# Two-layer kernel: C rows by DMA, the modulation product on GpSimd, and the last addition moved to the next stage

## What is computed

```python
h = layernorm(x) * (1 + ca) + sa
x = x + ga * state_space(h)
h = layernorm(x) * (1 + cb) + sb
x = x + gb * experts(h)
```

```python
h = exp(dt * A) * h + dt * u * B      # a scan over the 1024 tokens
y = sum_n(h * C) + u * D
out = (y * silu(z)) @ W_out.T + residual
```

## Time and profile before

| | us |
|---|---|
| median of 3 runs (4103.15 to 4108.57) | 4107.88 |
| span of the profiled execution, first to last instruction | 4108.2 |
| busy: TensorE, VectorE, ScalarE, GpSimd | 3305.6, 3549.2, 2321.0, 2624.4 |
| state-space stage, first scan to the last store | 2098.7 to 3914 |
| experts stage, first load to the end | 3918.9 to 4108 |

### The profile page before, as it was taken

The page is one execution under the profiler, slowest core; times in us unless marked ns, Lnnn a source line. Parts: engine busy times, 40 slices in busy tenths (PEclk is TensorE's granted clock), DMA queues, the critical chain, the costliest instruction groups (busy, mean ns, idle before and its releaser), DMA issues. The chain is left out here.

```text
span 4108.2 us, 61159 instructions
## 1 busy us (share of the span) xinstructions
PE 3305.6 (80%) x21708; PEld 1529.2 (37%) x21708; DVE 3549.2 (86%) x5829; ACT 2321.0 (56%) x4302; POOL 2624.4 (64%) x2459
## 2 busy tenths in 40 slices
PE   5979999999993999999566777777777777776467
PEld 3633333333332555555322232222232232222166
DVE  5768888888854999999359999999999999999967
ACT  5626666666672344444356666666666666666422
POOL 1102323232232888888369999999999999998723
PEclk8969999999996999999888888888888888887689
DMA  4894565655513111110112222212222222222132
GB/s 146 281 188 64 78 84 79 88 80 81 82 33 89 35 44 45 44 48 30 34 44 61 63 65 64 69 47 60 69 65 64 65 69 61 68 57 53 42 95 85
DMA packets 274957, 299.58 MB, mean 73 GB/s; under 512 B 35583, under 2 KB 205686, under 8 KB 274646
## 3 DMA queue, kind: packets, MB, share of 16 engines
q1 hardware_dynamic: 274654, 295.68, 31.4%
HBM read 210.22 MB, written 84.51 MB: 72 GB/s over the span
## 5 line engine op out<-in xcount | busy, mean ns | idle before, releaser
L1727 POOL TENSOR_TENSOR d_dBu<-d_dtu,d_Bn 128x1024 f32<-128x1024 f32 x512 | 1217.5, 2413 | 0.1
L1562 ACT ACTIVATE d_dA<-d_dt,d_decay 128x512 f32<-128x512 f32 x1024 | 690.9, 687 | 404.4 <-DVE d_h L1810 402.1
L752 ACT ACTIVATE b_P<-b_pT 128x512 f32<-128x512 f32 (+1 forms) x1120 | 571.8, 575 | 298.1 <-PE b_pT L658 295.3
L1810 DVE TENSOR_TENSOR_SCAN d_h<-d_dA,d_last_h,d_dBu 128x512 f32<-128x512 f32 x512 | 617.1, 1265 | 14.5 <-ACT d_dA L1562 12.8
L1810 DVE TENSOR_TENSOR_SCAN d_h<-d_dA,d_dBu 128x512 f32<-128x512 f32 x512 | 586.3, 1204 | 40.3 <-ACT d_dA L1562 39.0
L785 DVE CUSTOM_DVE_ANT_0 b_pS<-b_pS,mask_qk 128x512 f32<-128x512 f32 (+1 forms) x768 | 501.7, 690 | 83.6 <-PE b_pS L668 74.3
L630 POOL TENSOR_SCALAR_AFFINE_SELECT b_P<-b_P 128x128 f32<-128x128 f32 (+2 forms) x608 | 192.8, 321 | 515.0 <-ACT b_P L752 503.2
L668 PE MATMUL b_pS<-KS,QS 99*128 99x512 bf16 (+3 forms) x1536 | 475.0, 339 | 28.5 <-PEq L85 21.6
L658 PE MATMUL b_pT<-QS,KS 118*128 118x512 bf16 (+3 forms) x1536 | 449.1, 329 | 3.1 <-ACT b_P L752 2.1
L1817 DVE TENSOR_TENSOR d_h<-d_h,d_C 128x2048 f32<-128x2048 f32 x192 | 434.4, 2262 | 0.7 <-PE d_C L1446 0.7
L1446 PE MATMUL d_C<-d_bc,d_pick 96*128 96x512 bf16 x256 | 114.6, 448 | 396.1 <-DVE d_h L1817 396.1
(11 more groups left out here) (313 smaller groups left out, 5983.2 us busy)
## 6 DMA issues: line engine op xcount, KB each, us to landing
d_Bn<-scratch_bs SPq DMA_DIRECT2D x128, 512.0 KB, 4.9
scratch_parts<-a_part SPq DMA_DIRECT2D x48, 512.0 KB, 4.1
QS<-scratch_parts SPq DMA_DIRECT2D x192, 128.0 KB, 7.4
KS<-scratch_parts SPq DMA_DIRECT2D x192, 128.0 KB, 7.9
scratch_v<-a_v SPq DMA_DIRECT2D x16, 1024.0 KB, 7.7
V<-scratch_v SPq DMA_DIRECT2D x32, 512.0 KB, 11.7
a_x<-in_L_attn_x_dram SPq DMA_DIRECT2D x16, 512.0 KB, 7.7
scratch_o<-b_O SPq DMA_DIRECT2D x16, 512.0 KB, 10.0
```

Of the source, the lines that this page charges most:

```text
L752: act.activation(t[:, heads[0]:heads[-1] + 1, c * CH:c * CH + w], pT[:, place % RING, 0:len(heads) * w].rearrange("p (h w) -> p h w", w=w) ...
L1562: act.activation(dA[:, m % 2, :], dt[:, c.k % 2, m, :], ACT.Exp, scale=decay[:, m, n:n + 1]).then_inc(dA_d, 1)
L1727: pool.tensor_tensor(product(c, n)[:, 2 * j:2 * j + 2, :], dtu[:, c.k % 2, 2 * j:2 * j + 2, :], Bn[:, n // BG % 2, n % BG, :].unsqueeze(1) ...
L1810: dve.tensor_tensor_scan(h[:, n % HS, m, :], dA[:, m % 2, :], product(c, n)[:, m, :], start, ALU.mult, ALU.add).then_inc(scanned, 1)
```

## The change

1. C rows of GpSimd's four states. SyncE stores B and C rows to DRAM (`bs` now has 32 rows) and loads the four C rows repeated over 128 partitions into `Cn`, which has four places now. `evacuate_c` and the four C products of TensorE go.
2. `modulate` goes from VectorE, turn 4, to GpSimd, turn 6, directly ahead of `shift`. `stats` goes from turn 6 to turn 7, `scale_bias` from 8 to 9, and the second normalisation on ScalarE goes half a turn to a turn later.
3. `finish` goes. The gated output is stored as `a3`, and `experts` loads x2 and a3 and adds them on GpSimd (`join`); its loads run three chunks ahead, not two.

```diff
@@ state_space, SyncE
+            def spread_c(at, j):
+                row = NS + POOL_C[j]
+                sp.dma_start(Cn[:, j, :], S["bs"][row:row + 1, tokens(at)].to_broadcast([P, CH])).then_inc(cn_in[j], 16)
...
-                    sp.dma_start(S["bs"][:, tokens(q)], xb[DR:DR + NS, :]).then_inc(b_st, 16)
+                    sp.dma_start(S["bs"][:, tokens(q)], xb[DR:DR + 2 * NS, :]).then_inc(b_st, 16)
                 spread_next(c, 7)
                 if q is not None:
                     wait(sp, b_st, q.times(16, 16))
+                    for j in range(len(POOL_C) - 1):
+                        if c is not None:
+                            wait(sp, hC_pool, c.times(len(POOL_C), j + 1))
+                        spread_c(q, j)
                     for g in range(2):
                         if c is not None:
                             wait(sp, dBu_d, c.times(2 * NS, 2 * (NS - BG + BG * g)))
                         spread_b(q, g)
+                        if g == 0:
+                            if c is not None:
+                                wait(sp, hC_pool, c.times(len(POOL_C), len(POOL_C)))
+                            spread_c(q, len(POOL_C) - 1)
                 if e is not None:
-                    wait(sp, x3_d, e.times(1, 1))
-                    sp.dma_start(tiles(S["x3"][tokens(e), :]), x2e[:, :, :]).then_inc(stored, 16)
+                    wait(sp, ag_d, e.times(2, 2))
+                    sp.dma_start(tiles(S["a3"][tokens(e), :]), h1e[:, :, :]).then_inc(stored, 16)
...
-                    sp.dma_start(x2e[:, :, :], tiles(S["x2"][tokens(c), :])).then_inc(e_in, 16)
@@ state_space, TensorE
-                if n == 0:
+                if n in POOL_C:
+                    return
+                if n == DVE_C[0]:
...
-                if (n - 1) % NS in POOL_C:
-                    wait(pe, c_ev, c.times(len(POOL_C), POOL_C.index(n - 1) + 1))
-                else:
-                    wait(pe, hC_dve, c.times(len(DVE_C), sum(i < n for i in DVE_C)))
+                wait(pe, hC_dve, c.times(len(DVE_C), DVE_C.index(n)))
@@ state_space, ScalarE
-            def evacuate_c(c, n):
-                j = POOL_C.index(n)
-                wait(act, c_mm, c.times(NS, n + 1))
-                wait(act, hC_pool, c.times(len(POOL_C), j - 1))
-                act.activation(Cn[:, j % 2, :], pC[:, :], ACT.Copy).then_inc(c_ev, 1)
...
-                 {4: lambda f: normalise(f, 0, (2, 3)), 11: lambda f: normalise(f, 1, (1,)), 12: lambda f: normalise(f, 1, (3,)), 14: carry, 15: lambda f: turned(f, 1)}),
+                 {4: lambda f: normalise(f, 0, (2, 3)), 12: lambda f: normalise(f, 1, (1,)), 13: lambda f: normalise(f, 1, (3,)), 14: carry, 15: lambda f: turned(f, 1)}),
...
-                 {3: lambda f: normalise(f, 0, (0, 1)), 10: lambda f: normalise(f, 1, (0,)), 11: lambda f: normalise(f, 1, (2,)),
+                 {3: lambda f: normalise(f, 0, (0, 1)), 11: lambda f: normalise(f, 1, (0,)), 12: lambda f: normalise(f, 1, (2,)),
@@ state_space, GpSimd
-            def shift(f):
+            def modulate(f):
+                wait(pool, m_in[f.k // 2 % 2], f.over(4, 16, 16))
+                wait(pool, xn1, f.times(1, 1))
+                pool.tensor_tensor(x[:, :, :], x[:, :, :], row(f, CA), ALU.mult).then_inc(h_mul, 1)
...
-            def finish(e):
-                wait(pool, e_in, e.times(32, 32))
-                wait(pool, ag_d, e.times(2, 2))
-                pool.tensor_tensor(x2e[:, :, :], x2e[:, :, :], h1e[:, :, :], ALU.add).then_inc(x3_d, 1)
...
-                ({15: finish}, {14: step_input}, {6: shift, 8: scale_bias_first}))
+                ({}, {14: step_input}, {6: modulate, 9: scale_bias_first}))
@@ state_space, VectorE
-                 {4: modulate, 6: stats, 13: clear}))
+                 {7: stats, 13: clear}))
@@ experts, SyncE
-                sp.dma_start(x[:, n % XS, :, :], S["x3"][n * CH:(n + 1) * CH, :].rearrange("(t p) d -> p t d", p=P)).then_inc(x_in[n % XS], 16)
+                sp.dma_start(x[:, n % XS, :, :], S["x2"][n * CH:(n + 1) * CH, :].rearrange("(t p) d -> p t d", p=P)).then_inc(x_in[n % XS], 16)
+                wait(sp, x3_d, n - AS + 1)
+                sp.dma_start(a[:, n % AS, :, :], S["a3"][n * CH:(n + 1) * CH, :].rearrange("(t p) d -> p t d", p=P)).then_inc(x_in[n % XS], 16)
@@ experts, GpSimd
+            def join(n):
+                wait(pool, x_in[n % XS], n // XS * 32 + 32)
+                pool.tensor_tensor(x[:, n % XS, :, :], x[:, n % XS, :, :], a[:, n % AS, :, :], ALU.add).then_inc(x3_d, 1)
+
+            join(0)
...
                 if c is not None:
                     wait(pool, og_d, c + 1)
                     pool.tensor_tensor(x[:, c % XS, :, :], x[:, c % XS, :, :], og[:, c % 2, :, :], ALU.add).then_inc(out_d, 1)
+                if f is not None and f + 1 < total:
+                    join(f + 1)
@@ experts, VectorE
-                    wait(dve, x_in[f % XS], f // XS * 16 + 16)
+                    wait(dve, x3_d, f + 1)
```

More of the change, by code:

```diff
@@ L1489, in output @@
                 wait(pe, yz_d, e.times(1, 1))
-                wait(pe, e_in, e.times(32, 32))
+                wait(pe, e_in, e.times(16, 16))
                 for t in (2 * j, 2 * j + 1):
@@ L1710, in weigh @@
                 j = POOL_C.index(n)
-                wait(pool, c_ev, c.times(len(POOL_C), j + 1))
+                wait(pool, cn_in[j], c.times(16, 16))
                 wait(pool, scanned, c.times(NS * MD, MD * n + MD))
@@ L1836, in stats @@
                 last.then_inc(stat, 1)
-            def modulate(f):
-                wait(dve, m_in[f.k // 2 % 2], f.over(4, 16, 16))
-                wait(dve, xn1, f.times(1, 1))
-                dve.tensor_tensor(x[:, :, :], x[:, :, :], row(f, CA), ALU.mult).then_inc(h_mul, 1)
             def clear(f):
@@ L1946, in step @@
                     load(1)
-                if f is not None and f + 2 < total:
-                    load(f + 2)
+                    load(2)
+                if f is not None and f + 3 < total:
+                    load(f + 3)
                 if c is not None:
```

35 lines of the change are left out of this document (16 added, 19 removed).

## The result

| | kernel before | changed kernel |
|---|---|---|
| median of the runs | 4107.88 us | 4219.9 us |
| ratio, 95% interval | 1 | 1.027 (1.0255 to 1.0285) |
| span of the profiled execution | 4108.2 us | 4219.7 us |
| TensorE's mean granted clock | 0.898 | 0.881 |

The account below looks back on a forecast made before the run. VectorE was taken to bound the state-space stage and a loop of waits the experts stage. Terms: -8 (state-space), +49.9 (experts chain), +33 (clock), +4 (start) = +79 us on 4108.2, so 4187 us; range 4150 to 4212.

Parts of the forecast that it names:

- The experts chain: Experts stage: statistics wait for the join queued behind GpSimd's output addition; net 4.16 us a step, 12 steps, +49.9 us.
- Rival B: Experts stage: join ends before the gated product, step stays 10.05 us, state-space gain kept; 4075 to 4100, chance 0.04.
- The clock in the experts stage: Experts stage: TensorE's longer pause halves its clock for part of the output products; 2.75 us a step, +33 us.
- The statistics' cover: State-space stage: statistics moved to turn 7 no longer fill VectorE's wait for the decay; 1.81 us a chunk, +25.3 us.
- TensorE loses four C products a chunk, off the path: State-space stage: TensorE's dropped C products were taken to lie off the path, with no term in the sum.
- I cost it at nothing: State-space stage: GpSimd takes the modulation product and loses the last addition, staying at 209.5 of 225.3 us; cost 0.
- ScalarE's waits: State-space stage: VectorE's waits for ScalarE, 1.14 us a chunk on average, shrink as ScalarE gets lighter; -15.9 us if all go.
- the normalisation in turn 13: State-space stage: one ScalarE normalisation lands in turn 13 and makes ScalarE late; +7 us, between 0 and 12.
- the -7 of the middle piece: State-space stage, first to last gated product (7.5 pairs of chunks): predicted difference in span, -7 us.
- E: State-space stage: GpSimd becomes the bound, waiting for C or B rows; one us a chunk gives 4201, chance 0.04.
- Rival D: Experts stage: TensorE's clock stays at half for all the output products; 12 x 2.71 us more, 4219, chance 0.05.

Follow-up runs that it names:

- e9_old_c: Changed kernel with the join first and statistics in turn 6, C rows of GpSimd's states again made by TensorE's products and ScalarE's evacuations: 4094.5 us.
- e11_mod_only: Kernel before with only the modulation product moved to GpSimd in turn 6 and the normalisations one turn later: 4096.7 us.
- e8_mod_back: Changed kernel with the join first, and modulation product (VectorE, turn 4), statistics and normalisations as before the change: 4125.2 us.

## Why the prediction was wrong, and where it was right

**The experts chain** (49.9) was right, and right for its reason: with the join first the 85 us go, and 31.6 of them are the clock's. Rival B named the point that decides, a join that ends ahead of the gated product; the run with the join first puts it there and gets the step of 10.05.

**The clock in the experts stage** (33) was right: 31.6. The Trainium skill, TensorE: Matmul & The Clock Gate, Part 1, says that for modelling the ramp's penalty is under 1% of a typical kernel's span and that one should not fit a specific count of slow products; a forecast that leaves the term out on that ground is 33 us lower. The trace agrees on the size, 31.6 us being 0.7% of the span, but that is over a quarter of what the change cost.

**The statistics' cover** (+25.3): the step was right in kind, and in size by the trace. Turn 7 waits 4.05 us in the pair read (3.7 in most) instead of 0.37, where I had 3.62 more. Undoing it gave 40 us by the medians (37 to 40 with the join first), more than the cover, since convolutions and splits moved too; and in four pairs of seven turn 7 still waits 2.2 us or more with the statistics in turn 6, so the cover did not come back whole.

**The step that failed** is "TensorE loses four C products a chunk, off the path", put at nothing. I had the rows with which to doubt it: a pause of 3.15 us at which the clock holds and one of 4.71 at which it has fallen. With less for TensorE to do around them the pauses are 3.28 to 3.52 us in the changed kernel and up to 3.71 with the statistics in turn 6, the convolution behind takes 1.7 us more, and the scan of turn 3 waits 3.5 us a pair: +25 us. That it takes the C rows is shown: put back through TensorE and ScalarE they remove the waits of turn 3 from every pair, and in the kernels that have them there (before, e9_old_c, e11_mod_only) the first convolution is slow in none of 42 chunks. The other way is shown less cleanly: e8_mod_back brings the waits of turn 3 to the kernel before, though not in every pair, but it has the moved last addition as well. That the waits go by the clock is shown by the repeats. Why the clock recovers before the convolution in some chunks and not in others (with the C rows through ScalarE there are pauses of 3.37 and 3.61 us too, and the first convolution is at full speed) stays open. I applied the rule of the clock to the stage where I saw a new pause and not to the one where I removed work.

**The second is "I cost it at nothing"** of GpSimd's exchange of one addition for one product. GpSimd's busy time did not grow, and nobody waits for it by a semaphore, so by waits the cover held. But its instructions lie otherwise in time, and VectorE's splits, 4 a pair, end only behind them: +3.5 us a pair, again 25 us, by the pair's sum. That part is luck of phase: the four splits of a pair took 4.8 us before, 8.3 to 8.7 after, 7.5 or 8.2 with the statistics in turn 6.

**ScalarE's waits** were undersized as a gain: -15.9 and +7 were forecast; nearly all of them went (-3.45 a pair, 24 us), and the normalisation in turn 13 cost nothing. With these 15 us, 3 of the scans' busy time less the gate's wait, and the two terms of 25, the -7 of the middle piece become about +25. The runs with the join first and with the filled pause have the same stage and show 1699.4 and 1699.9, which is +26; in the profiled execution of the changed kernel the first pair was 4 us shorter.

The range's upper end, 4212, rested on E with one us a chunk, at 0.04. The loss was 2 us a chunk above the forecast: I bounded what the trace named and left no room for terms that it did not name. Rival D's 4219 is the measured time by luck: it has TensorE at half speed for all the output products, and the step shows them back at 1.03 us before it ends.

## What to carry to other kernels

Put work into an in-order queue at the place from which its inputs are there, not where the code reads well: one join behind an addition cost 85 us more than the same join ahead of it. When a change takes work off an engine that "has time", look at how long that engine's pauses become, and at every instruction of another engine that shares a resource with it; busy sums hide both. And undo each part by itself: here one of three parts held all the gain that these runs can show. Where the pairs of a trace differ, read several before you price one.

## What the runs showed of the hardware

**Short pauses of TensorE can cost clock, and one pause does not settle it.** At the turn of a chunk the products ran at full speed behind pauses of 2.81, 2.90 and 3.15 us and at half behind those of 3.47 and 3.71. Behind 3.28 us the sum took 1.15 us in the changed kernel and 2.02 in a chunk of the one with twelve repeats. Behind 3.52 us the sum was fast in both; the input products behind it took 3.57 us in the first and 1.98 in the second. And in the changed kernel a convolution fell to half speed behind a pause of 2.01 us, with the dead C products one behind 2.02. A clock that has fallen also makes the next pause shorter, since the work ahead of it takes longer: 2.01 us in the chunk where it had fallen, 3.47 where it had not. So removed work costs in jumps: the same convolution took 3.70 or 5.40 us.

**A VectorE instruction with two inputs from SBUF waits for GpSimd's running instruction.** A split of 32x512 takes 0.68 us beside an idle GpSimd (the one that writes float32), and 1.09, 2.32 and 4.72 us (the one that writes bfloat16) beside a GpSimd instruction that ends 0.54, 1.78 and 4.19 us after its start: each time it ends some 0.54 us behind it. The profile books this as busy time of VectorE, not as a wait. The Trainium skill, SBUF — State Buffer, section "SBUF: two separate sides", states it: the two engines share a pair of ports, which the one that starts first holds for its whole instruction, if VectorE's has two SBUF inputs. The trace agrees, with the numbers above. The scans and the C products of VectorE, which read one operand from PSUM, keep their length in all these kernels (1.20 to 1.26 and 2.26 us).
